# A two-layer adapter kernel: the early weight tile, the low-rank factor and the loads at the pass switch reordered

## What is computed

```python
x = x + L0(x)                              # x: 8 x 256 x 1024, 2048 tokens
x = x + L1(x)

def L0(x):                                 # a weight of 1024 x 1024, quantised on the fly
    delta = (lora_B @ lora_A) * 0.5        # rank 64
    cb = codebook / max(|codebook|)        # 8 levels
    scale = exp(scale_log)                 # one per row and group of 128 columns
    n = (weight + delta) / scale
    q = cb[searchsorted((cb[:-1] + cb[1:]) / 2, n)]
    return x @ (((q - n) + n) * scale + delta).T

def L1(x):                                 # F = 2752; rank-16 adapters, one picked per batch row
    gate = x @ W_gate.T + 0.5 * (x @ A_gate[b].T) @ B_gate[b].T
    up   = x @ W_up.T   + 0.5 * (x @ A_up[b].T)   @ B_up[b].T
    act  = silu(gate) * up
    return act @ W_down.T + 0.5 * (act @ A_down[b].T) @ B_down[b].T
```

## Time and profile before

| | |
|---|---|
| median of three runs | 1642.22 us (1639.8 to 1643.66) |
| profiled execution, its own time | 1641.95 us |
| its span | 1640.4 us |
| TensorE busy | 1595.8 us, 97% of the span |
| VectorE, ScalarE, GpSimd busy | 1284.3, 572.9, 528.8 us |
| granted TensorE clock, mean | 0.99 |

### The profile page before, as it was taken

The page is one execution under the profiler, slowest core; times in us unless marked ns, Lnnn a source line. Parts: engine busy times, 40 slices in busy tenths (PEclk is TensorE's granted clock), DMA queues, the critical chain, the costliest instruction groups (busy, mean ns, idle before and its releaser), DMA issues.

```text
span 1640.4 us, 21380 instructions
## 1 busy us (share of the span) xinstructions
PE 1595.8 (97%) x7032; PEld 1300.8 (79%) x7032; DVE 1284.3 (78%) x1727; ACT 572.9 (35%) x1024; POOL 528.8 (32%) x399
## 2 busy tenths in 40 slices
PE   4999999999999999998999999999999999999999
PEld 3878887788888888766788888888778888888887
DVE  6899968788888899877887889999766576685353
ACT  4511125433333333345333333333343333233231
POOL 4230011355555555554444455556410000000000
PEclk8999999999999999998999999999999999999999
DMA  9473264466667777784446777876357777686563
GB/s 286 103 128 92 84 200 100 102 161 158 166 156 168 178 179 174 180 244 130 115 114 133 171 166 178 185 176 172 97 172 187 170 197 177 153 229 203 152 192 117
DMA packets 381452, 264.41 MB, mean 161 GB/s; under 512 B 228640, under 2 KB 302368, under 8 KB 381216
## 3 DMA queue, kind: packets, MB, share of 16 engines
q1 hardware_dynamic: 299072, 229.31, 53.8%
q10 hardware_dynamic: 80192, 27.94, 7.1%
q0 software_dynamic: 2080, 5.80, 1.8%
HBM read 167.84 MB, written 89.36 MB: 157 GB/s over the span
## 4 chain that ended last, share of the span: by engine, by line
PE 82%; DVE 14%; issue 2%; DMA 1%; ACT 1%; SPq 0%; DVEq 0%; ACTq 0%
PE bank L1746 20%; PE bankC L1746 14%; PE bankA L1746 14%; PE bank L1973 10%; PE bankA L1973 6%; PE bankC L1973 6%; PE bankT L1973 3%; DVE qsum L1542 2%; DVE xl L1257 1%; PE bankT L1793 1%; PE bankT L1794 1%; PE bankC L1758 1%; DVE qa L1527 1%; PE bank L1775 1%; DVE ts L1350 1%
## 5 line engine op out<-in xcount | busy, mean ns | idle before, releaser
L957 ACT CAST rh<-wt 128x512 fp32r<-128x512 f32 (+1 forms) x308 | 187.8, 611 | 446.3 <-PE bankA L1758 99.2
L1248 DVE TENSOR_TENSOR rl<-wt,rh 128x512 fp32r<-128x512 f32 (+1 forms) x308 | 280.9, 917 | 7.3 <-ACT rh L957 7.2
L1411 DVE TENSOR_TENSOR ll<-ll,lh 128x512 fp32r<-128x512 f32 (+1 forms) x154 | 108.2, 703 | 154.9 <-ACT lh L1066 154.4
L1746 PE MATMUL bank<-xh,rl 128*128 128x512 f32 (+1 forms) x528 | 205.7, 390 | 0.0
L1746 PE MATMUL bank<-xl,rh 128*128 128x512 f32 (+1 forms) x528 | 205.7, 390 | 0.0
L1746 PE MATMUL bank<-xh,rh 128*128 128x512 f32 (+1 forms) x528 | 205.7, 390 | 0.0
L1066 ACT CAST lh<-ll 128x512 fp32r<-128x512 f32 (+1 forms) x154 | 95.5, 621 | 269.4 <-DMA ll<-LT_d 264.1
L824 POOL TENSOR_TENSOR wt<-wt 128x512 f32<-128x512 f32 (+1 forms) x44 | 57.6, 1309 | 318.5 <-DVE wt L1242 318.5
L1746 PE MATMUL bankC<-xh,rh 128*128 128x512 f32 (+1 forms) x352 | 137.7, 391 | 2.2 <-DVE xl L1257 2.2
L1746 PE MATMUL bankC<-xl,rh 128*128 128x512 f32 (+1 forms) x352 | 137.8, 391 | 0.0
L1746 PE MATMUL bankC<-xh,rl 128*128 128x512 f32 (+1 forms) x352 | 137.7, 391 | 0.0
(11 more groups left out here) (207 smaller groups left out, 3597.6 us busy)
## 6 DMA issues: line engine op xcount, KB each, us to landing
ll<-LT_d SPq DMA_DIRECT2D x148, 256.0 KB, 2.9
wn<-in_L_cond_W_gate_dram SPq DMA_DIRECT2D x80, 256.0 KB, 5.4
wn<-in_L_cond_W_up_dram SPq DMA_DIRECT2D x80, 256.0 KB, 5.1
RT_d<-dt SPq DMA_DIRECT2D x70, 256.0 KB, 3.2
ql<-RT_d SPq DMA_DIRECT2D x70, 256.0 KB, 3.6
LT_d<-ev ACTq DMA_DIRECT2D x60, 256.0 KB, 2.6
dn<-in_L_cond_W_down_dram SPq DMA_DIRECT2D x86, 128.0 KB, 3.8
LT_d<-s2a SPq DMA_DIRECT2D x40, 256.0 KB, 4.2
```

The lines of the kernel that those rows point to most:

```text
L957: nc.scalar.copy(rh[:, v % RING, 0:KH * rows], wsrc(RSRC[p], rows)).then_inc(s_hi, 1)
L1248: dv.tensor_tensor(rl[:, v % RING, 0:KH * rows], wsrc(RSRC[p], rows), rh[:, v % RING, 0:KH * rows].bitcast(f32), ALU.subtract).then_inc(s_ ...
L1411: dv.tensor_tensor(ll[0:rows, n % NL, :], ll[0:rows, n % NL, :].bitcast(f32), lh[0:rows, n % NL, :].bitcast(f32), ALU.subtract).then_inc(s ...
L1746: last = te.matmul(OUT[p][0:rows, :], a[:, u % RING, cols], b[:, OPND[p], k, :], start=k == 0 and n == 0, stop=k == KH - 1 and n == 2 and ...
```

## The change

- The weight tiles, and the scale of tile 0, are loaded by one transfer each in place of four; the scale of the other tiles follows behind two token loads, with an exponential and a reciprocal of its own.
- VectorE makes the codebook's constants before it waits for `lb` of tile 0.
- The identity is added to `bankD` by four matmuls of 32 columns per tile on TensorE (`ident_add`, -2 times -1, halved later with delta) and no longer to `eff`.
- 20 token pieces are made before the first main product, 12 between the products.
- `LATER` becomes 12 steps (5 for the last tile); `adapters_lo` moves to the beginning of a later tile, `store_adapters` with it.
- `ts`: the mask is applied when the factor is copied and summed; then four full-width copies, two subtractions, and two copies of the result (`ts_dup`). The first factor is begun one product earlier.
- At the pass switch the token operands are split one product earlier, matrix 23 is loaded behind the seventh piece, and its four transposes stand two products later.

```diff
-XFIRST = 2 * KD
-QS = 22
+XFIRST = 20
+QS = 21
...
-LATER = KD
+LATER = {o: 12 if o < KD - 1 else 5 for o in range(1, KD)}
...
+LATE_W = 7 * (NM // 2 + 1)
...
         def load_weight(o):
-            for i in range(NI):
-                sp.dma_start(lw[i * Q:(i + 1) * Q, :], weight[i * DI + o * Q:i * DI + (o + 1) * Q, :]).then_inc(s_lw, 16)
+            sp.dma_start(lw[:, :], weight.rearrange("(i o r) d -> i o r d", i=NI, r=Q)[:, bass.ds(o, 1), :, :]
+                         .rearrange("i o r d -> i (o r) d")).then_inc(s_lw, 16)
...
-        for i in range(NI):
-            sp.dma_start(scale[i * Q:(i + 1) * Q, :, :],
-                         scale_log[i * DI:(i + 1) * DI].rearrange("(o r) g u -> r o (g u)", r=Q)).then_inc(s_cb, 16)
+        sp.dma_start(scale[:, 0, :], scale_log.rearrange("(i o r) g u -> i o r (g u)", i=NI, r=Q)[:, bass.ds(0, 1), :, :]
+                     .rearrange("i o r g -> i (o r) g")).then_inc(s_sc, 16)
...
         load_nat(2)
         load_nat(3)
+        for i in range(NI):
+            sp.dma_start(scale[i * Q:(i + 1) * Q, 1:KD, :],
+                         scale_log[i * DI + Q:(i + 1) * DI].rearrange("(o r) g u -> r o (g u)", r=Q)).then_inc(s_scr, 16)
         sp.wait_ge(s_trL, 1)
...
-                if i == (BUILD[o] + LATER) // KD and o < KD - 1:
+                if i == (BUILD[o] + LATER[o]) // KD and o < KD - 1:
                     if o + 3 < KD:
                         sp.wait_ge(s_trL, o + 3)
                         load_lb(o + 3)
                     load_adapters(o)
-                if i == (BUILD[o] + 28) // KD and o < KD - 1:
-                    store_adapters(o - 1)
+                if i == (BUILD[o] + 5) // KD and o > 1:
+                    store_adapters(o - 2)
             store_x1(i)
...
-            if p == 3 and 0 <= mm + 2 < NM:
+            if p == 3 and 0 <= mm + 2 < NM and mm != NM // 2 - 1:
                 load_wn(mm + 2)
             if 7 * (NM // 2 - 1) <= u < 7 * (NM // 2):
                 load_x(u - 7 * (NM // 2 - 1))
+            if u == 7 * (NM // 2) - 1:
+                load_wn(NM // 2 + 1)
...
-            nc.scalar.copy(tx[:, :], (bankC[:, 1, :], bank1[:, :])[t][2 * CR:4 * CR, :]).then_inc(s_tq, 1)
+            for b in range(CB):
+                part = slice(b * SEQ, (b + 1) * SEQ)
+                ins = nc.scalar.activation(tx[:, part], (bankC[:, 1, :], bank1[:, :])[t][2 * CR:4 * CR, part], ACT.Copy,
+                                           scale=half_of[2 * CR:4 * CR, b:b + 1])
+            ins.then_inc(s_tq, 1)
...
             for i in range(4):
-                g = slice(i % 2 * CR, (i % 2 + 1) * CR)
-                for b in range(CB):
-                    part = slice(b * SEQ, (b + 1) * SEQ)
-                    ins = nc.scalar.activation(ts[i * CR:(i + 1) * CR, t, i % 2, part], tx[g, part], ACT.Copy,
-                                               scale=half_of[g, b:b + 1])
-            ins.then_inc(s_tq, 1)
+                ins = nc.scalar.copy(ts[i * CR:(i + 1) * CR, t, i % 2, :], tx[i % 2 * CR:(i % 2 + 1) * CR, :])
+                if i == 1:
+                    ins.then_inc(s_th, 1)
+
+        def ts_dup(h, t):
+            act.wait_ge(s_tlo, 2 * h + t + 1)
+            for g in range(2):
+                ins = nc.scalar.copy(ts[(3 - g) * CR:(4 - g) * CR, t, g, :], ts[(1 - g) * CR:(2 - g) * CR, t, g, :].bitcast(f32))
+            ins.then_inc(s_ts, 1)
...
-        for i in range(NI):
-            act.dma_start(lw[i * Q:(i + 1) * Q, :], weight[i * DI:i * DI + Q, :]).then_inc(s_lw0, 16)
+        act.dma_start(lw[:, :], weight.rearrange("(i o r) d -> i o r d", i=NI, r=Q)[:, bass.ds(0, 1), :, :]
+                      .rearrange("i o r d -> i (o r) d")).then_inc(s_lw0, 16)
...
-        act.wait_ge(s_cb, 16 * (1 + NI))
-        nc.scalar.activation(scale[:, :, :], scale[:, :, :], ACT.Exp).then_inc(s_exp, 1)
+        nc.scalar.activation(minus2[:, :], ident[:, :], ACT.Copy, scale=-2.0).then_inc(s_neg1, 1)
+        act.wait_ge(s_sc, 16)
+        nc.scalar.activation(scale[:, 0, :], scale[:, 0, :], ACT.Exp).then_inc(s_exp, 1)
         nat_hi(0)
         for u in range(XFIRST):
             nat_lo(u, XFIRST)
             if u == KD:
                 lb_hi(1)
+            if u == KD + 2:
+                act.wait_ge(s_scr, 16 * NI)
+                nc.scalar.activation(scale[:, 1:KD, :], scale[:, 1:KD, :], ACT.Exp).then_inc(s_exp, 1)
         w_hi(0)
         nat_hi(XFIRST)
...
-            if 7 * (NM // 2) - 3 <= u < 7 * (NM // 2) + 4:
-                x_hi(1, u - 7 * (NM // 2) + 3)
+            if 7 * (NM // 2) - 4 <= u < 7 * (NM // 2) + 3:
+                x_hi(1, u - 7 * (NM // 2) + 4)
             if live and m == 1 and p == 4:
                 a_hi(4 * it)
+            if mm in (0, NM // 2) and p in (2, 6):
+                ts_copy(mm // (NM // 2), p // 6)
             if mm in (0, NM // 2) and p in (3, 6):
-                ts_copy(mm // (NM // 2), p // 6)
+                ts_hi(mm // (NM // 2), p // 6)
             if mm in (0, NM // 2) and p == 4:
-                ts_hi(mm // (NM // 2), 0)
+                ts_dup(mm // (NM // 2), 0)
             if mm in (1, NM // 2 + 1) and p == 0:
-                ts_hi(mm // (NM // 2), 1)
+                ts_dup(mm // (NM // 2), 1)
...
-            dv.tensor_tensor(tx[:, :], (bankC[:, 1, :], bank1[:, :])[t][0:2 * CR, :], tx[:, :], ALU.add).then_inc(s_tc, 1)
+            for b in range(CB):
+                part = slice(b * SEQ, (b + 1) * SEQ)
+                ins = dv.scalar_tensor_tensor(out=tx[:, part], in0=(bankC[:, 1, :], bank1[:, :])[t][0:2 * CR, part],
+                                              scalar=half_of[0:2 * CR, b:b + 1], in1=tx[:, part],
+                                              op0=ALU.mult, op1=ALU.add)
+            ins.then_inc(s_tc, 1)
 
         def ts_lo(h, t):
-            dve.wait_ge(s_tq, 2 * (2 * h + t) + 2)
-            block = [slice(i * CR, (i + 1) * CR) for i in range(4)]
-            for i in range(4):
-                g = (i + 1) % 2
-                for b in range(CB):
-                    part = slice(b * SEQ, (b + 1) * SEQ)
-                    ins = dv.scalar_tensor_tensor(out=ts[block[i], t, g, part], in0=tx[block[g], part],
-                                                  scalar=half_of[block[g], b:b + 1],
-                                                  in1=ts[block[g], t, g, part].bitcast(f32),
-                                                  op0=ALU.mult, op1=ALU.subtract)
-            ins.then_inc(s_ts, 1)
+            dve.wait_ge(s_th, 2 * h + t + 1)
+            for g in range(2):
+                mine = slice(g * CR, (g + 1) * CR)
+                ins = dv.tensor_tensor(ts[(1 - g) * CR:(2 - g) * CR, t, g, :], tx[mine, :], ts[mine, t, g, :].bitcast(f32),
+                                       ALU.subtract)
+            ins.then_inc(s_tlo, 1)
...
-        dv.tensor_copy(lbT[:, 0, :], bankB(0)).then_inc(s_lb0, 1)
-        dve.wait_ge(s_lb0, 1)
-        lb_lo(0)
-        dve.wait_ge(s_cb, 16 * (1 + NI))
+        dve.wait_ge(s_cb, 16)
...
+        dve.wait_ge(s_trL, 1)
+        dv.tensor_copy(lbT[:, 0, :], bankB(0)).then_inc(s_ophi, 1)
+        dve.wait_ge(s_ophi, 2)
+        lb_lo(0)
...
+        settle(dv.reciprocal(rscale[:, 0, :], scale[:, 0, :]))
+
+        def quantise(o, begin, early, mid, late):
...
+                dve.wait_ge(s_lw, 16 * o)
+            begin()
...
-            n = QS - 6
+            n = QS - 5
...
+            dve.wait_ge(s_idn, o + 1)
             for h in range(2):
                 chain(dv.scalar_tensor_tensor(out=eff[:, h * HALF:(h + 1) * HALF], in0=bankD[h], scalar=SCALE0,
                                               in1=qa[:, h * HALF:(h + 1) * HALF], op0=ALU.mult, op1=ALU.add))
             after(n + 5)
-
-            for i in range(NI):
-                q = slice(i * Q, (i + 1) * Q)
-                dg = eff[q, i * DI + o * Q:i * DI + (o + 1) * Q]
-                ins = dv.tensor_tensor(dg, dg, ident[q, q], ALU.add)
-            chain(ins)
-            after(n + 6)
...
+        def rest_of_scale():
+            dve.wait_ge(s_exp, 2)
+            settle(dv.reciprocal(rscale[:, 1:KD, :].rearrange("p o g -> p (o g)"),
+                                 scale[:, 1:KD, :].rearrange("p o g -> p (o g)")))
+
+        quantise(0, lambda: None, lambda: None, lambda: None, rest_of_scale)
         lb_lo(1)
+
+        def begin_of(o):
+            if o > 2:
+                adapters_lo(o - 3)
...
-            if o > 1:
-                adapters_lo(o - 2)
 
         for o in range(1, KD):
-            quantise(o, lambda: early_of(o), lambda: mid_of(o), lambda: late_of(o))
+            quantise(o, lambda: begin_of(o), lambda: early_of(o), lambda: mid_of(o), lambda: late_of(o))
+        adapters_lo(KD - 3)
...
-                if v % 7 == 0 and 0 <= v // 7 < NM:
+                if v - 2 == LATE_W if v // 7 == NM // 2 + 1 else v % 7 == 0 and 0 <= v // 7 < NM:
...
+            if mm in (0, NM // 2) and p == 2:
```

(56 more changed lines are left out.)

1 line of the change is left out of this document (removed).

## The result

The median was 1638.1 us over 20 runs (1634.8 to 1643.0), against 1641.6 for the kernel before over 20 runs on the same chips: ratio 0.9978, 95% interval 0.9970 to 0.9987. The change is 0.2% faster; the forecast was 0.8%.

A forecast was written before the change was run, and what follows sets the result against it. TensorE, busy 1595.8 of 1640.4 us, was taken as the bound, its 44.6 us idle the prize. Terms +1.3 - 3.2 - 9.2 - 2.0 = -13.1 gave a median of 1629, range 1619 to 1638.

The forecast's parts named there:

- Start: +1.3: Up to the second weight tile: later early loads outweigh fewer token groups; tile taken at 69.3 instead of 68, +1.3 us.
- The start costs more: Rival at the start: first token pieces share four engines with the first tile; start +5, total 1635 to 1639, chance 0.18.
- if cb and the first slice of scale land near 10: VectorE's chain at the start: constants and first products end near 13, 6 us earlier, 6.8 with the identity addition gone.
- The first rival: At the start: the single-transfer weight tile uses all engines, first product near 40, start -7, total 1621; chance 0.20.
- First stage: Weight-tile stage: waits for `eff` shrink from 3.9 to 0.3 us, identity matmuls on TensorE add 2.1; -3.2 us.
- Start of the main stage: TensorE's waits of 3.86 and 2.46 us for `ts` go, with their clock loss, leaving 0.5; -9.2 us.
- itself plus 1.7 us of clock: Price of each removed TensorE wait of 1.7 to 3.9 us: its length plus 1.7 us of reduced clock behind it.
- Pass switch: Near 750 us: late matrix leaves one `ts` wait of some 8 us, later waits go; -2.0, between +2 and -7.

## Why the prediction was wrong

**The failed step** is the term "Start: +1.3", in the sentence "All the early loads had landed near 35 + 5 x 0.71 = 38.5; now near 46.3". Measured: `lb` of tile 2 at 53.8, the first main product at 55.63 (forecast 48.3), the second tile at 76.10 (69.3). That is +8.1 in the profiled execution in place of +1.3. Within this term the price of the single transfers is what failed: the forecast with them (1629) lies 8 us above its own case without them (1621), and the runs lie 18.7 apart. The rival "The start costs more" had the place right ("the copies of ScalarE begin at 17 to 25": 25.56), but its +5 was too small as well.

Two assumptions under the term were wrong. First, "if cb and the first slice of scale land near 10": they landed at 20.3 and 21.8, with tile 0 under way from 0.94 on (10.5 and 13.5 with four transfers). I had priced each engine by itself, 96 KB more on four of them, 4.4 us, and let the other loads run at the full rate. The rate of the whole DMA fell to 202 GB/s, at a full share, while such a tile ran. The packets show that this is no matter of four engines alone: in 8 to 13 us the changed kernel moves 625 packets, the one with four transfers 1114, at the same share, and by the trace's DMA records the 2 KB packets of the token pieces take 167 ns at the median instead of 85. Nine in ten of them take 149 or more, which the four engines of the tile alone can't explain. And SP's queue, which the forecast lets run on, stands still behind the tile, so that the second `lb` is issued 14.2 us later. Second, for the same reason the bytes were the wrong measure of a tile. From "near 40" with all engines to 48.3 the forecast has 8.3 us for both tiles; the runs show 15.1, 8.4 for tile 0 and 6.7 for tile 1. The number of engines was right: a share of 0.26 and 85 GB/s alone, so the rule cited from the Trainium skill ("DMA: Bandwidth & Descriptors", on why a DMA increments its semaphore by 16) agrees with the trace on the number; which engines they are, no view shows. What a transfer on four engines does to its neighbours neither that rule nor a row told.

**The first rival** (all engines, first product near 40, 1621, chance 0.20) describes the kernel with four transfers: 40.51 and 1619.45. With them the forecast of the whole was right within 2 us, though its start gained 8.1 us and not 7.

**First stage: -3.2 forecast, -2.1 measured.** The waits for `eff` are 0.3, as forecast. An identity step stands 0.36 us in TensorE's stream (forecast 0.3):

```profile
62.91 0.51 PE L1888 MATMUL bank<-minus,minus 128*128 128x32 f32 x4
63.27 0.66 PE L1863 MATMUL bankA<-ident,nat 128*128 128x128 f32 x4
```

What is missing is mostly a new wait, again by the single transfer. A store of the adapters stands behind weight tile 4 in SP's queue, and ScalarE waits for it:

```profile
102.92 0.58 SPq L634 DMA_DIRECT2D lw<-in_L_cond_weight_dram  x1
...
104.53 0.62 SPq L683 DMA_DIRECT2D BdT_d<-bd_st  x1
...
119.59 0.43 ACT L1127 CAST at_st<-bankC 128x128 fp32r<-128x128 f32 x2 [8.13 <-DMA BdT_d<-bd_st]
...
120.73 0.50 PE L1914 MATMUL bankT<-lxh,lwh 128*128 128x512 f32 x1 [1.05 <-ACT x1t_st L1119]
```

Here that costs TensorE 1.05 us. Six such waits of ScalarE are 27.3 us in all; with four transfers there are two, 14.6 us. In three other kernels whose tiles 1 to 7 come in single transfers TensorE waits 2.3, 2.6 and 3.2 us at this place, and the stage takes 183.60, 185.55 and 186.30 us, against 182.89 here; in the six with four transfers it takes 181.4 to 181.8. So part of what the changed kernel loses at its median is likely lost here and not at the start. With four transfers alone the second tile is taken at 59.93 and the main stage starts at 241.51, 181.58 us, against 184.94 before: -3.4, the forecast -3.2. The edit of the identity itself is worth nothing in that kernel (1620.34 against 1619.45), though the prediction counted the removed waits as its gain: with the addition on VectorE 2.5 us of them stay, and the eight steps of TensorE cost 2.9. That the rest of the waits went because the constants and `adapters_lo` have moved is likely, but no run takes these apart.

**Start of the main stage: -9.2 forecast, -9.2 measured**, and -9.2 with this edit alone. Here the price of a removed wait, itself plus 1.7 us of clock, held: in 253 to 312 before, the granted clock is 0.94 over 59 us, 3.5 us lost, and in 259 to 309 of the changed kernel it is 1.00.

**Pass switch: -2.0 forecast, -3.2 measured.** The mechanism is the forecast one, row by row: the matrix lands at 743.8 (747.2), the third transpose ends at 753.7 (758.3), ScalarE casts S2 at 756.4 (760.9), `ts` comes at 758.4 (762.6), one wait of 7.8 us (8). That the sum came out near is partly luck. The prediction didn't credit the edits one by one: the new `ts` and the earlier token copies are worth 3.6 and 3.9 us, the late matrix is a loss of 2.2 to 4.3 inside that gain, and the +1.0 of the longer wait for `ad` in front of the stretch isn't in the 3.2.

**The range.** The median, 1638.1, lies 0.1 us outside 1619 to 1638. The dear start ended at 1639, and I cut the range at 1638 because I gave that case too little: a transfer form that no row showed for 512 KB deserved more than 0.18.

## What to carry to other kernels

Count on how many engines a transfer runs before merging several into one: here SP's 1.7 us for four issues became 0.6 for one, and 18.7 us were lost (7.3 in the kernel before). A transfer on few engines has to be priced with what travels beside and behind it, stores that another engine waits for included, not by its own bytes. And an edit with several parts is worth taking apart: one part here, the chain of `ts`, was worth 14.7 us alone, four times the whole.

## What the hardware did that I had not expected

- A load of 512 KB of the four-group form beside token pieces takes the whole DMA from 388 GB/s (four transfers) to 202, at busy shares of 1.06 and 1.07. Alone it moves 85 GB/s at a share of 0.26. Its neighbours slow down on the other engines too: their 2 KB packets take 167 ns at the median in 8 to 13 us, 169 in 41 to 47, and 85 with four transfers. Why is not settled: the experiment with `lb` in four transfers (219 GB/s) only shows that the small loads' own form is not the cause.
- SP's queue stands still behind it: two token pieces took 12.70 us to issue, 3.02 with four transfers.
- The beginning of the main stage varies between executions: 258.99 and 264.86 in two kernels with single transfers that are equal up to it, 241.3 to 241.8 in five with four transfers and 245.6 in a sixth. That sixth is late at its first main product already (42.90); behind the second tile all six take the same time within 0.4 us, those with single transfers 182.9 to 186.3.
